# Forming the differences of a 16-bit split on TensorE instead of GpSimd, in the node stage ahead of attention

## The chip, the cores and the metric
One core of a Trainium2 chip runs the whole program in one launch. The metric is the device time of one execution in microseconds (us), where lower is better. A core has five engines with in-order instruction streams: TensorE (PE: matmuls and transposes, results go to PSUM), VectorE (DVE), ScalarE (ACT), GpSimd (POOL) and SyncE (SP, which issues DMAs). They are ordered only by semaphores that the kernel writes out by hand.

## The reference, cut to what matters
A network of two layers over 3125 nodes of 256 channels and 50000 edges. The change lies between the mixture of experts of layer 0 and the residual sum behind the attention of layer 1:

```python
# layer 0: y = x + (two chosen experts, weighted); then a layer norm with gamma and beta is added
x = x + (layernorm(y) * gamma + beta)
# layer 1, attention over edges, on the normalized nodes
h = (layernorm(x) @ W.T).reshape(n, 8, 32)
alpha = (h[src] * a_src).sum(-1) + (h[dst] * a_dst).sum(-1)
alpha = alpha + (relu(edge_attr @ edge_W.T + edge_b) * h[dst]).sum(-1)
...
x = x + segment_sum(h[src] * attn) + bias
x = x + ffn(layernorm(x))
```

## The kernel before
The nodes are padded to NT = 25 tiles of P = 128 rows, one row per partition, in TURNS = 5 turns of TB = 5 tiles. The program is a row of blocks with a barrier of all engines between two; inside a block every engine has its own function. `nodes1` (the stage in front of attention) is one such block, `attention` is the next, and `hidden1` (last node stage and first half of the feed-forward network) the one behind.

In `nodes1` the engines do this. SP issues the loads (three per turn: the results of the two experts and the normalized nodes, 640 KB each), between them three broadcasts of small vectors (`a_src`, `a_dst`, bias), and then the stores of 25 finished rows. DVE: the products that append the attention columns to the weights (L1484, L1485), then `combine(c)` of a turn (weighted sum of the loads, L1453 and L1454, and statistics), `update(c)` (L1464, L1465: the normalized sum is added to x, and statistics of x) and `offsets(c)` (L1472), in the order combine(0), combine(1), update(0), and then for each turn c: combine(c+2), offsets(c), update(c+1). ACT takes square roots (`root`, L906) for both norms, normalizes five tiles at once (`apply`, L1544) when offsets(c) is done, and then, tile by tile, copies the transposed tile out of PSUM (`copy_turned`, L1551), copies the product out (`take`, L1558) and makes three 16-bit parts of it. PE transposes each tile (`turn`, L1508) and multiplies it with the weights (`project`, L1517, 272 columns, f32).

The three parts are: part 0 is the row rounded to bf16 (L1560, from the copied row in SBUF, so it waits for that copy); the first difference, row minus part 0, is formed by GpSimd (`rests`, L1615) or, in the last turn, by DVE (`late_rests`, L1478); part 1 is that rounded (L1564); the second difference is formed by GpSimd (`lefts`, L1619); part 2 is that rounded (L1568, a whole turn later). The parts go to `hparts`, which attention reads; the row goes to a table in DRAM, from which attention gathers.

GpSimd also adds beta to all of x ahead of the turns (L1605, five instructions of 128x1280), adds the bias of attention's output to x after each turn's five tiles (`with_bias`, L1609, 128x1280) and clears the turn's part of `acc` (L1622), into which attention writes and which served as a load buffer until then. ACT issues `again.root(c + 1)` behind the five tiles of turn c, and offsets(c+1) on DVE waits for it: so a turn's tiles on ACT and PE lie in a ring with the next turn's offsets.

In `hidden1` (turns of CT = 4 tiles) DVE runs nodes(0), nodes(1), normalized(0), and then alternates. `nodes(c)` is per tile: attention's sums times the inverse denominator (L1771), added to x (L1773), statistics (L890). PE starts with the transposes of the first normalized tile (L1802), then the large products (L1811).

## Time and profile before
| | us |
|---|---|
| median of 3 runs | 2664.62 (2662.47 to 2669.9) |
| the profiled execution | 2668.54 |
| its span, first to last instruction | 2666.6 |
| of it `nodes1`, 1367 to 1520.4 | 153.4 |
| `attention`, 1520.4 to 2194.7 | 674.3 |
| `hidden1` up to 2345 | 150.3 |

All later times are microseconds from the start of the span. The median of the runs is 3.9 us below the profiled execution, 0.15% of it. Busy time of an engine counts the union of its instructions; "x4" is a count of instructions.
### The profile page before, as it was taken

The page shows a single profiled execution, that of the slowest core. Times are in us where ns is not written, and L with a number is a line of the kernel's source. Part 1 is how long each engine was busy: PE and PEld are TensorE (multiplying, and loading weights), DVE is VectorE, ACT ScalarE, POOL GpSimd, SP SyncE. Part 2 cuts the span into 40 slices and gives each one's busy share as a digit, 9 for nine tenths or more (in the row PEclk, how much of TensorE's full clock was granted, in tenths as well). Part 3 has the DMA queues.
Part 4 walks back from the last instruction along what each step waited for, and adds up shares of the span by engine and source line. Part 5 has one row for each costly group of instructions (what it writes and reads, how often), then busy time and mean ns, then how long its engine had stood idle before and what let it go on. Part 6 is the DMA issues. An engine that isn't in the chain of part 4 may idle for free. (4 is left out here: it accounts for less than half of the span.)

```text
span 2666.6 us, 41224 instructions
## 1 busy us (share of the span) xinstructions
PE 1931.2 (72%) x12513; PEld 1491.1 (56%) x12602; DVE 1654.7 (62%) x3320; ACT 918.3 (34%) x2309; POOL 1266.6 (47%) x1252
## 2 busy tenths in 40 slices
PE   3366666666269987499942578888888878969994
PEld 1245444444247765399931356666666652329994
DVE  8555555555257768655559589999999986031222
ACT  7333333323100002133313645555555543423331
POOL 0377777777710000155543577777777740002221
PEclk9678787777679998699976699999999998979997
DMA  2355554544478861522250255555555535000113
GB/s 78 104 183 188 193 175 167 179 162 164 146 270 284 293 223 50 177 70 72 70 183 21 87 153 160 163 158 162 161 164 162 162 91 174 18 8 31 38 38 112
DMA packets 192123, 366.13 MB, mean 137 GB/s; under 512 B 47573, under 2 KB 102632, under 8 KB 191525
## 3 DMA queue, kind: packets, MB, share of 16 engines
q1 hardware_dynamic: 135472, 207.05, 24.0%
q0 software_dynamic: 56160, 156.43, 18.6%
q8 instruction: 106, 1.74, 0.3%
q14 instruction: 111, 0.91, 0.1%
q10 hardware_dynamic: 274, 0.00, 0.0%
HBM read 232.23 MB, written 131.07 MB: 136 GB/s over the span
## 5 line engine op out<-in xcount | busy, mean ns | idle before, releaser
L1970 POOL DMA_INDIRECT att_rows<-hdram,top_ix x488 | 499.0, 1023 | 149.8 <-issue 147.7
L839 POOL DMA_INDIRECT mtab<-first_w,msgs_ix x308 | 308.2, 1001 | 93.9 <-issue 89.0
L708 PE MATMUL msgs_p_m<-nodes_n,msgs_hott 128*128 x976 | 316.3, 480 | 40.0 <-issue 31.0
L2040 PE MATMUL att_p_acc<-att_msg,att_hot 128*128 128x264 f32 x976 | 249.4, 400 | 77.2 <-ACT att_msg L2085 54.7
L708 PEld LDWEIGHTS msgs_p_m<-nodes_n,msgs_hott 128*128 128x128 f32 x976 | 221.3, 238 | 92.3 <-issue 56.2
L1141 POOL IOTA route_column<- 128x50 f32 (+1 forms) x2 | 0.3, 171 | 524.8 <-ACTq L1137 524.8
L2040 PEld LDWEIGHTS att_p_acc<-att_msg,att_hot 128*128 128x128 f32 x976 | 177.1, 191 | 119.7 <-DVE att_msg L2207 59.9
L1341 PE MATMUL exp_y<-exp_own,exp_ht 128*128 128x256 f32 x1032 | 239.0, 379 | 2.4 <-issue 2.4
L2070 ACT ACTIVATE att_enc<-att_p_z 128x1024 f32<-128x1024 f32 x122 | 124.8, 1023 | 298.3 <-PE att_p_z L1983 298.3
L839 POOL DMA_INDIRECT mtab<-msgs_rw,msgs_ix x180 | 181.6, 1009 | 72.7 <-issue 52.1
L1341 PEld LDWEIGHTS exp_y<-exp_own,exp_ht 128*128 128x128 f32 x1032 | 188.5, 190 | 24.7 <-issue 3.1
L607 DVE TENSOR_TENSOR first_w<-msgs_p_m,msgs_sorted 128x1024 f32<-128x1024 f32 x77 | 94.3, 1224 | 151.5 <-PE msgs_p_m L708 142.5
L1364 ACT COPY exp_xt<-exp_turned 128x256 f32<-128x256 f32 x97 | 36.1, 372 | 359.2 <-PE exp_turned L1320 359.2
L1285 DVE COPY exp_own<-ffn_w 128x2048 f32 x32 | 39.3, 1227 | 190.0 <-PE exp_y L1341 188.1
L2158 DVE TENSOR_TENSOR att_enc<-att_enc,att_p_h 128x1024 f32<-128x1024 f32 x122 | 148.7, 1218 | 12.8 <-PE att_p_h L1993 9.8
L2160 DVE TENSOR_REDUCE att_al<-att_enc 128x32 f32<-128x1024 f32 x122 | 148.8, 1220 | 4.2
L2207 DVE TENSOR_TENSOR att_msg<-att_rows,att_ex 128x1024 f32<-128x1024 f32 x122 | 148.8, 1219 | 1.1
L743 PE MATMUL msgs_p_m<-first_w,msgs_hott 128*128 128x256 f32 x616 | 143.2, 386 | 1.1 <-issue 0.3
L772 ACT CAST msgs_hott<-msgs_p_hot 128x512 f32<-128x512 bf16 x122 | 71.4, 585 | 179.3 <-PE msgs_p_hot L698 172.9
L1331 PEld LDWEIGHTS exp_hidden<-exp_xt,exp_own 128*128 128x128 f32 x1040 | 127.8, 194 | 4.5 <-issue 1.3
L1331 PE MATMUL exp_hidden<-exp_xt,exp_own 128*128 128x128 f32 x1040 | 128.3, 277 | 1.0 <-DVE exp_own L1277 1.0
L743 PEld LDWEIGHTS msgs_p_m<-first_w,msgs_hott 128*128 128x128 f32 x616 | 110.9, 189 | 32.2 <-issue 17.7
(390 smaller groups left out, 3966.3 us busy)
## 6 DMA issues: line engine op xcount, KB each, us to landing
first_w<-mtab SPq DMA_DIRECT2D x77, 520.0 KB, 4.6
etab<-msgs_et SPq DMA_DIRECT2D x122, 288.0 KB, 2.3
att_hz<-etab SPq DMA_DIRECT2D x122, 288.0 KB, 3.0
msgs_rw<-mtab SPq DMA_DIRECT2D x45, 520.0 KB, 4.7
first_w<-in_L_ffn_w SPq DMA_DIRECT2D x16, 512.0 KB, 4.6
ffn0x_w<-in_L_ffn_w SPq DMA_DIRECT2D x16, 512.0 KB
ffn_w<-in_L_ffn_Wd SPq DMA_DIRECT2D x8, 1024.0 KB, 12.1
att_rows<-hdram,top_ix POOLq DMA_INDIRECT x488, 3.2
```

Of the source, the lines that this page charges most:

```text
L607: V.tensor_tensor(rw[g % RS][:, :, 0:C], p_m[g % 2][:], bc(rows[:, g % SR, :, 6], 2, C), ALU.mult).then_inc(s_rw, 1)
L708: last = T.matmul(p_m[g % 2][:, q, :], hott[g % 2][:, q, :], node, start=True, stop=True)
L743: last = T.matmul(p_m[g % 2][:, 0, :], hott[g % 2][:, q, :], rw[g % RS][:, q, 0:C], start=(q == 0), stop=(q == G - 1))
L839: nc.gpsimd.indirect_dma_start(mtab, bass.IndirectOffsetOnAxis(ap=ix[:, g, q:q + 1], axis=0), rw[g % RS][:, q, :], None).then_inc(s_free[g ...
L1331: last = T.matmul(hidden[t % 2][:, f * P:(f + 1) * P], own1[:, k, f * P:(f + 1) * P], xt[t % 2][:, k * P:(k + 1) * P], start=(k == 0), sto ...
L1341: last = T.matmul(y[t % 2][:, 0:C], ht[t % 2][:, f, :], own2[:, f, :], start=(f == 0), stop=(f == FC - 1))
L1970: nc.gpsimd.indirect_dma_start(rows[:, g % RS, q, :], None, hdram, bass.IndirectOffsetOnAxis(ap=ix1[:, g, q:q + 1], axis=0)).then_inc(s_ro ...
L2040: last = T.matmul(p_acc[g % 2][:, 0:HW], hot[g % 2][:, q, :], msg[g % 2][:, q, :], start=(q == 0), stop=(q == G - 1))
L2070: S.activation(enc[g % 2][:], p_z[:], ACT.Relu).then_inc(s_enc, 1)
L2158: V.tensor_tensor(e[:], e[:], p_h[:], ALU.mult).then_inc(s_prod, 1)
L2160: V.tensor_reduce(al[t % 2][:, j * G:(j + 1) * G, :].rearrange("p q h -> p (q h)"), e[:].rearrange("p q (h d) -> p (q h) d", h=H), AX, ALU ...
L2207: V.tensor_tensor(msg[g % 2][:].rearrange("p q (h d) -> p q h d", d=D + 1)[:, :, :, 0:D], rows[:, g % RS, :, 0:C].rearrange("p q (h d) -> ...
```

## The change
The stage's split is reordered, and its pieces change engines:

- `rests`, `late_rests`, `lefts`, `with_bias` and `clear` leave GpSimd and DVE. GpSimd keeps only the five additions of beta.
- PE forms both differences in PSUM: `less_first(i)` is identity times row (f32) plus minus-identity times part 0 (bf16), `less_second(i)` is the same with parts 0 and 1 subtracted, in one bank (`p_left`), so it waits for the third part of the tile before. The bf16 matrix `minus` is made once by DVE.
- ACT reads the row's part 0 out of PSUM instead of out of the copied row, and the second and third part out of PSUM too; the third part follows three tiles behind, across turns, not a turn later. ACT also clears `acc`, one tile a time (`clear`, 128x264).
- PE's loop runs two tiles further and ACT's three, as a pipeline over all 25 tiles.
- On DVE combine(0) and combine(1) now come ahead of the products for the weights.
- The bias is loaded at the head of `hidden1` and added there by DVE, one more 128x256 addition per tile in `nodes`, which waits for that load once.

```diff
-            row_broadcast(sp, bi[:], A["L1_gnn_bias"], s_bi)
...
             V.memset(none[:], 0.0).then_inc(s_none, 1)
+            V.tensor_scalar(minus[:], cst["ident"][:], -1.0, None, ALU.mult).then_inc(s_minus, 1)
+            combine(0)
+            combine(1)
             dve.wait_ge(s_av, 32)
...
-            combine(0)
-            combine(1)
...
-            for i in range(LASTC, NT):
-                late_rests(i)
...
                 if i >= 2:
-                    pe.wait_ge(s_row, i - 1)
+                    pe.wait_ge(s_first, i - 1)
...
+            def less_first(i):
+                pe.wait_ge(s_first, i + 1)
+                if i >= 2:
+                    pe.wait_ge(s_second, i - 1)
+                T.matmul(p_less[i % 2][:, 0:HN], cst["ident"][:], row[i % 4][:, 0:HN], start=True, stop=False)
+                T.matmul(p_less[i % 2][:, 0:HN], minus[:], hparts[:, i, 0, :], start=False, stop=True).then_inc(s_less, 1)
+
+            def less_second(i):
+                pe.wait_ge(s_second, i + 1)
+                if i:
+                    pe.wait_ge(s_third, i)
+                T.matmul(p_left[0][:, 0:HN], cst["ident"][:], row[i % 4][:, 0:HN], start=True, stop=False)
+                T.matmul(p_left[0][:, 0:HN], minus[:], hparts[:, i, 0, :], start=False, stop=False)
+                T.matmul(p_left[0][:, 0:HN], minus[:], hparts[:, i, 1, :], start=False, stop=True).then_inc(s_left, 1)
...
-            for i in range(NT):
-                if i % TB < TB - 1:
+            for i in range(NT + 2):
+                if i % TB < TB - 1 and i + 1 < NT:
                     turn(i + 1)
-                project(i)
+                if i < NT:
+                    project(i)
+                if 0 <= i - 1 < NT:
+                    less_first(i - 1)
+                if 0 <= i - 2 < NT:
+                    less_second(i - 2)
...
                 S.copy(row[i % 4][:], p_o[i % 2][:, 0:HP]).then_inc(s_row, 1)
-                act.wait_ge(s_row, i + 1)
-                S.copy(hparts[:, i, 0, :], row[i % 4][:, 0:HN]).then_inc(s_first, 1)
+                S.copy(hparts[:, i, 0, :], p_o[i % 2][:, 0:HN]).then_inc(s_first, 1)
...
+            for i in range(NT + 3):
+                c, b = i // TB, i % TB
+                if b == 0 and i < NT:
+                    if c + 2 < TURNS:
+                        norm.root(act, S, c + 2)
+                    for k in range(TB):
+                        apply(c * TB + k)
+                if i < NT:
                     copy_turned(i)
+                if 0 <= i - 1 < NT:
+                    take(i - 1)
+                if 0 <= i - 2 < NT:
+                    second(i - 2)
+                if 0 <= i - 3 < NT:
+                    third(i - 3)
+                if b == TB - 1 and c + 1 < TURNS:
                     again.root(act, S, c + 1)
+                if i < NT:
+                    clear(i)
...
         @block.sync
         def _(sp):
+            row_broadcast(sp, bi[:], A["L1_gnn_bias"], s_bi)
             sp.dma_start(flat[:], A["L1_ffn_b1"].rearrange("(f p) -> f p", p=P)).then_inc(s_in, 16)
...
+                    link(V.tensor_tensor(to[:], to[:], bi[:], ALU.add))
                     link(V.tensor_tensor(x[:, i, :], x[:, i, :], to[:], ALU.add))
...
             link(V.reciprocal(den[:], den[:]))
+            dve.wait_ge(s_bi, 16)
             nodes(0)
```

## Rows read from the trace of the kernel before

**Rows 1.** Busy time by stage: stretch, length; busy us (x instructions) per engine; PEclk, DMA, GB/s.
```profile
1367.00:1520.40 153.40, 49.68 (x154) 33.71 (x154) 116.10 (x245) 58.43 (x162) 66.13 (x60) 0.61 0.27 90
1520.40:2194.70 674.30, 538.84 (x5097) 418.40 (x5186) 604.24 (x899) 350.41 (x704) 498.98 (x488) 0.98 0.54 156
```

**Rows 2.** Timeline, head of nodes1: start, duration, engine, line, operation, out<-in, [idle before].
```profile
1367.77 14.67 POOL L1605 TENSOR_TENSOR top_x<-top_x,wts_be 128x1280 f32<-128x1280 f32 x5 [4.79 <-POOLq L87]
1376.77 2.94 DVE L1484 TENSOR_TENSOR upd_tmp<-upd_w,upd_av 128x512 f32<-128x512 f32 x1 [8.63 <-DMA upd_av<-in_L_gnn_a_dst]
...
1383.87 0.48 DVE L1453 SCALAR_TENSOR_TENSOR sum_acc<-upd_got,wts_wt,sum_acc 128x256 f32<-128x256 f32 x1 [0.16 <-DVE upd_w L1485]
```

**Rows 3.** Timeline: update(0) begins on DVE; then apply(0) on ACT and update(1) on DVE.
```profile
1401.70 0.48 DVE L1464 SCALAR_TENSOR_TENSOR sum_acc<-sum_acc,upd_norm_mean,wts_ga 128x256 f32<-128x256 f32 x1
...
1419.72 2.57 ACT L1544 ACTIVATE upd_n<-top_x,upd_again_mean,upd_again_t 128x256 f32<-128x256 f32 x5
1419.82 0.49 DVE L1464 SCALAR_TENSOR_TENSOR sum_acc<-sum_acc,upd_norm_mean,wts_ga 128x256 f32<-128x256 f32 x1
```

**Rows 4.** Timeline, DVE and POOL behind the first turn's tiles.
```profile
1434.13 3.16 DVE L1453 SCALAR_TENSOR_TENSOR sum_acc<-upd_got,wts_wt,sum_acc 128x256 f32<-128x256 f32 x1
1434.13 2.88 POOL L1609 TENSOR_TENSOR top_x<-top_x,upd_bi 128x1280 f32<-128x1280 f32 x1
```

**Rows 5.** Timeline, from apply(3) to the last instruction of nodes1.
```profile
1484.12 2.08 ACT L1544 ACTIVATE upd_n<-top_x,upd_again_mean,upd_again_t 128x256 f32<-128x256 f32 x4 [2.98 <-DVE upd_again_mean L1472]
...
1498.17 0.20 ACT L906 ACTIVATE upd_again_t<-upd_again_var 128x5 f32<-128x5 f32 x1
...
1498.63 2.69 DVE L1472 SCALAR_TENSOR_TENSOR upd_again_mean<-upd_again_mean,upd_again_t 128x5 f32<-128x5 f32 x1
...
1501.36 2.56 ACT L1544 ACTIVATE upd_n<-top_x,upd_again_mean,upd_again_t 128x256 f32<-128x256 f32 x5 [2.98 <-DVE upd_again_mean L1472]
...
1504.23 2.18 PE L1517 MATMUL upd_p_o<-upd_w,upd_xt 128*128 128x272 f32 x4 [1.04 <-ACT upd_xt L1551]
...
1519.51 0.41 ACT L1568 CAST heads_parts<-upd_rest 128x264 bf16<-128x264 f32 x1 [0.23 <-POOL upd_rest L1619]
```

**Rows 6.** Timeline, costs of one piece: PE at full clock, and ACT back to back.
```profile
1428.41 0.38 PE L1508 MATMUL upd_p_t<-top_ident,upd_n 128*128 128x128 f32 x2
...
1428.63 1.08 PE L1517 MATMUL upd_p_o<-upd_w,upd_xt 128*128 128x272 f32 x4
...
1477.06 0.41 ACT L1564 CAST heads_parts<-upd_rest 128x264 bf16<-128x264 f32 x1
1477.37 0.36 ACT L1551 COPY upd_xt<-upd_p_t 128x256 f32<-128x256 f32 x1
...
1701.81 2.05 PE L2040 MATMUL att_p_acc<-att_msg,att_hot 128*128 128x264 f32 x8 [0.76 <-DVE att_msg L2207]
...
1704.43 1.47 PE L1993 MATMUL att_p_h<-wts_logits,att_hz 128*128 128x256 bf16 x12
```

**Rows 7.** Timeline of PE: the first matmul after an idle stretch in attention.
```profile
1543.38 0.33 PE L2009 MATMUL att_p_top<-top_ident,att_al 128*128 128x128 f32 x1 [3.58 <-DVE att_al L2173]
```

**Rows 8.** Busy time and granted clock right behind that idle stretch.
```profile
1544.00:1545.00 1.00, 1.00 (x4) 0.37 (x3) 0.96 (x2) 0.09 (x1) 0.70 (x2) 0.50 0.34 110
```

**Rows 9.** Timeline, hidden1: SP's first load, the first tile on DVE, PE's first transposes.
```profile
2194.73 0.35 SPq L1750 DMA_DIRECT2D hid_flat<-in_L_ffn_b  x1
...
2196.60 0.42 DVE L1771 TENSOR_TENSOR hid_part<-sum_acc,hid_den 128x256 f32<-128x256 f32 x1
...
2197.06 0.42 DVE L1773 TENSOR_TENSOR top_x<-top_x,hid_part 128x256 f32<-128x256 f32 x1
...
2210.87 2.33 PE L1802 MATMUL hid_p_t<-top_ident,nodes_n 128*128 128x128 f32 x8 [8.40 <-DVE nodes_n L914]
```

**Rows 10.** Busy time in hidden1 once PE runs.
```profile
2220.00:2345.00 125.00, 125.00 (x310) 39.49 (x309) 27.63 (x90) 49.48 (x81) 0.00 (x0) 1.00 0.14 48
```

**Rows 11.** The 25 stores of rows in nodes1 (132 KB each), from issue to landing.
```profile
DMA to landing us min/median/max: 1.7/1.7/3.7
```

More of the change, by code:

```diff
@@ L1396, in nodes1 @@
     n2 = [a.sb(f"n2{s}", [P, TB, C]) for s in two]
-    w, av, bi = a.sb("w", [P, KC, HP]), a.sb("av", [P, 2, C]), a.sb("bi", [P, C])
+    w, av, minus = a.sb("w", [P, KC, HP]), a.sb("av", [P, 2, C]), a.sb("minus", [P, P], BF16)
     tmp, none = a.sb("tmp", [P, KC, C]), a.sb("none", [P, HR])
@@ L1400, in nodes1 @@
     row = [a.sb(f"row{s}", [P, HP]) for s in range(4)]
-    rest = [a.sb(f"rest{s}", [P, HN]) for s in range(TB)]
     p_w = a.ps("p_w", [P, KC, C])
-    p_t, p_o = ([a.ps(f"{m}{s}", [P, 512]) for s in two] for m in ("p_t", "p_o"))
+    p_t, p_o, p_less, p_left = ([a.ps(f"{m}{s}", [P, 512]) for s in range(k)] for m, k in (
+        ("p_t", 2), ("p_o", 2), ("p_less", 2), ("p_left", 1)))
     norm, again = Norm(a, "norm"), Norm(a, "again")
-    (s_av, s_chain, s_none, s_pw, s_w, s_wa, s_shift, s_n, s_t, s_xt, s_o, s_row, s_first, s_rest, s_late, s_second, s_left,
-     s_third, s_zero, s_bi, s_sum, s_be, s_acc) = (a.sem(m) for m in (
-         "av", "chain", "none", "pw", "w", "wa", "shift", "n", "t", "xt", "o", "row", "first", "rest", "late", "second",
-         "left", "third", "zero", "bi", "sum", "be", "acc"))
+    (s_av, s_chain, s_none, s_pw, s_w, s_wa, s_shift, s_n, s_t, s_xt, s_o, s_row, s_first, s_less, s_second, s_left,
+     s_third, s_zero, s_be, s_clear, s_minus) = (a.sem(m) for m in (
+         "av", "chain", "none", "pw", "w", "wa", "shift", "n", "t", "xt", "o", "row", "first", "less", "second", "left",
+         "third", "zero", "be", "clear", "minus"))
     s_got, s_out = [a.sem(f"got{c}") for c in range(TURNS)], [a.sem(f"out{s}") for s in range(4)]
-    def rest_ready(eng, i):
-        if i < LASTC:
-            eng.wait_ge(s_rest, i + 1)
-        else:
-            eng.wait_ge(s_late, i - LASTC + 1)
     with nc.Block() as block:
@@ L1574, in _ @@
             again.root(act, S, 0)
-            for c in range(TURNS):
-                if c + 2 < TURNS:
-                    norm.root(act, S, c + 2)
-                for b in range(TB):
-                    apply(c * TB + b)
-                for b in range(TB):
-                    i = c * TB + b
-                    copy_turned(i)
-                    if b:
-                        take(i - 1)
-                    if c:
-                        third(i - TB)
-                    if b >= 2:
-                        second(i - 2)
-                take((c + 1) * TB - 1)
-                for b in range(TB - 2, TB):
-                    second(c * TB + b)
-                if c + 1 < TURNS:
+            act.wait_ge(s_none, 1)
@@ L1593, in _ @@
                     again.root(act, S, c + 1)
-            for i in range(LASTC, NT):
-                third(i)
+                if i < NT:
+                    clear(i)
+            act.wait_ge(s_clear, NT)
         @block.gpsimd
         def _(pool):
-            G_ = nc.gpsimd
-            def chunk(c):
-                return x[:, c * TB:(c + 1) * TB, :]
-            def first_offset(c):
-                G_.tensor_tensor(chunk(c), chunk(c), bc(wts["be"][:], 1, TB), ALU.add).then_inc(s_be, 1)
@@ L1621, in clear @@
-            def clear(c):
-                nc.gpsimd.memset(acc[:, c * TB:(c + 1) * TB, :], 0.0).then_inc(s_acc, 1)
-            for c in range(TURNS):
-                first_offset(c)
-            pool.wait_ge(s_bi, 16)
-            for i in range(NT):
-                if i < LASTC:
-                    rests(i)
-                if i >= 2:
-                    lefts(i - 2)
-                if i % TB == TB - 1:
-                    with_bias(i // TB)
-                    clear(i // TB)
-            for i in range(NT - 2, NT):
-                lefts(i)
@@ L1737, in hidden1 @@
         "chain", "in", "b1", "bt", "n", "t", "xt", "h", "ht", "g", "flip", "l"))
-    s_store = a.sem("store")
+    s_store, s_bi = a.sem("store"), a.sem("bi")
     def tiles(c):
```

33 lines of the change are left out of this document (10 added, 23 removed).

## The prediction
> **What bounds the kernel now.** I read the busy time by stage first [rows 1]. The change touches nodes1 (153.4 us) and hidden1; attention between them keeps its code. In nodes1 the reader is to see that no engine but DVE is near full: 116.1 of 153.4 us, against PE 49.7, ACT 58.4 and POOL 66.1, and that PE's mean clock is 0.61.
>
> The timeline of the stage tells why. Undisturbed, DVE needs 18.12 us from the start of update(0) to the start of update(1), which is one update, one combine and one offsets [rows 3]. From the first apply at 1419.72 to the last conversion, ended at 1519.92, there are 100.2 us [rows 3, 5]. Part of this is DVE being stretched: while POOL adds the bias to five tiles (2.88 us), DVE's addition of 256 columns, 0.48 us elsewhere, takes 3.16 and ends just behind POOL's [rows 2, 4]. The same happens to the last offsets, an instruction on 5 columns that takes 2.69 us, and ACT waits for it for 2.98 us [rows 5]. The last turn then runs from 1501.36 to 1519.92, 18.6 us, with GpSimd and DVE in its chain.
>
> So the stage is DVE with GpSimd's interference for the first three turns, and for the last two the ring of ACT, PE and GpSimd: the root at 1498.17 frees offsets(4), which frees the last turn.
>
> In hidden1, DVE works through eight tiles before PE's first transpose at 2210.87, and PE is then busy 125 of 125 us [rows 9, 10]. What is added on DVE ahead of 2210.87 moves the end; what is added behind is covered by PE.
>
> **The change part by part.** Call S(c) the moment at which apply(c) starts on ACT. Before, S(0) is 1419.7 and S(4) 1501.4 [rows 3, 5].
>
> *Start on DVE.* combine(0) need not wait for the broadcast of a_dst any more, only for the first three loads. They were issued ahead of it on the same queue, and the product waited until 1376.77 for the broadcast [rows 2]; I take 1376.8 for combine(0). But POOL's additions of beta run until 1382.44 (five, some 2.9 each), and rows 2 show what that does: the product issued at 1376.77 takes 2.94, one per addition of POOL. Two of the combine's additions get through by 1383.0, 1.0 us of work. Before, combine(0) started at 1383.87, so DVE is 0.9 + 1.0 = 1.9 ahead. The products and reductions for the weights now stand behind combine(1), undisturbed. A pair of them took 1.43 (from POOL's end at 1382.44 to 1383.87), so 2.8 for two, between combine(1) and update(0). S(0) comes 2.8 - 1.9 = 0.9 later, at 1420.6. The `minus` matrix falls into time in which DVE waits for loads. PE needs the weights only after S(0), so their later place costs nothing else.
>
> *DVE's turns.* With no bias, no difference and no clear on GpSimd, DVE runs at 18.1 per turn. S(1) = 1438.7, S(2) = 1456.8, if the ring of ACT and PE is not slower. The bounds are 18.1 and, with a root that comes late, the ring's time below. From S(2) to S(3) and from S(3) to S(4) DVE has only an update (about 9 us, half of 18.1) and waits for the root of the turn before: the ring decides.
>
> *TensorE's new work.* Per tile at full clock, from rows 6: two transposes 0.38; project 1.08; each f32 matmul of 264 columns is two of the instructions that took 2.05 for eight, 0.51; each bf16 one of 256 columns 1.47/12 = 0.12. less_first is 0.51 + 0.12 = 0.63, less_second 0.51 + 0.25 = 0.76. Sum 2.85. No row shows f32 and bf16 weights taking turns within one sum; the bounds are 0 (project and transposes follow each other in rows 6 with no gap, 0.22 between their starts) and 0.76, the idle that a wait for DVE's product cost in attention [rows 6]. I take 0.15, nearer to the closely packed rows: 3.0 per tile, where turn and project alone were 1.46.
>
> *ScalarE's.* Two instructions back to back start 0.31 apart [rows 6]. Per tile six of them (turned tile, row, three parts, clear), 1.9 us, and 0.51 of apply: 2.4 per tile, below PE's 3.0 and covered by it. In the pipeline each part waits for something that PE did an iteration earlier, and less_second's wait for the third part of the tile before finds it done while PE does the next transposes, product and first difference (2.1 us). Queued behind that wait on PE are the next tile's transposes; ACT's copy of them would be the first to feel it.
>
> *The ring.* From S(c) to the first project 2.87 (five applies and a copy) [rows 5]. Then 2.5 for that iteration without its transposes, three more tiles at 3.0, and 1.5 for the third part, root, reciprocal and offsets: T = 2.87 + 2.5 + 9.0 + 1.5 = 15.9. In S terms it is 4x + 3.9 with x the tile. Before, from apply(3) at 1484.12 to the root it took 14.1 us, and 3.2 more passed until apply(4), most of it behind GpSimd's addition [rows 5]: T replaces 17.3. S(3) = 1472.7, S(4) = 1488.6.
>
> *The tail.* 2.87 + 2.5 + 3 x 3.0 + 2.6 (the last tile has no transposes) = 17.0, then two more differences of the pipeline's end 1.4, a wait for the second part 0.2, the last difference 0.76 and the third part 0.6: 20.0. Stage end 1508.6 against 1519.92: **11.3 us less**.
>
> *The clock.* The first project of the last turn runs at half speed (2.18 against 1.08) [rows 5, 6], since PE had been idle long before it. An idle of 3.58 us in attention, and the clock was at 0.50 in the microseconds after it [rows 7, 8]; after an idle of 0.76 it was full [rows 6]. In the changed stage PE ends a turn's pieces 2.87 + 2.5 + 4 x 3.0 = 17.4 after S(c). While DVE sets the pace (18.1) it then idles 1.3 until the first apply is through (0.6), works 0.4 on the transposes and idles 1.8 until project; where the ring sets the pace (15.9) it still holds 1.5 us of the turn before and idles only 1.0. A start at the lower level lasted at most from 1422.6 (S(0) + 2.87) to the full-speed transposes at 1428.41 [rows 3, 6], 5.8 us of which half is lost; I take 2.5. I take the first start cold (hidden: its turn has fewer differences and DVE bounds it) and the last two warm.
>
> The Trainium skill (TensorE: Matmul & The Clock Gate, What's actually happening and HAM oscillation) says that the array falls back to 1.2 GHz when it goes idle, and that loops with a wait in each round can start every round cold. By it this change, which fills PE's gaps, would either cure that here or pay it with twice the work; that it pays is the second rival, priced from rows.
>
> *The bias in hidden1.* One more addition per tile at 0.46 start to start [rows 9]; eight tiles stand before PE's first transpose: 3.7. The other 17 fall into DVE's idle time beside a PE that is full [rows 10]. The load: DVE wants it at 2196.60; SP issues first at 2194.73 and a DMA of its size landed 1.7 to 3.7 after its issue [rows 9, 11], so the wait is 0 to 1.9; I take 0.7, near the median. Behind it on SP's queue the other loads slip by some 0.4, and PE had got them and sat idle for 8.40 before the first transposes [rows 9]. Together **4.4 us more**.
>
> *Sum.* -11.3 + 4.4 = -6.9. The profiled execution (2668.54; span 2666.6) would become 2661.6, and on the median scale, 3.9 lower, 2664.6 - 6.9 = **2657.7**.
>
> **The rivals.**
> 1. *TensorE's tile is cheaper and the stage gains more.* x = 2.85 makes T 15.3, so the end falls by 3 x 0.6, and the bias's wait may be 0: -6.9 - 1.8 - 0.7 = -9.4, 2655.2. If in addition GpSimd's additions did not hold combine(0), S(0) would be 5 earlier: 2650. The rows for the latter speak against it (2.94 us).
> 2. *The clock falls at every turn.* T becomes 18.4, the tail 22.5: S(2) 1457.1, S(4) 1493.9, end 1516.4; the stage gains 3.5, the bias takes 4.4: +0.9, 2665.5. For it: two idle stretches near each other at each head. Against it: neither is as long as the 3.58 of rows 7.
> 3. *TensorE becomes the bound, the slower end.* The end is S(1) + 3T + T + 4.1. It equals the old end less 4.4 when T is about 18.1; from there on the whole is slower than before, 0.4 us per 0.1. That takes a tile of 3.55 warm. At a tile of 3.55 and cold starts T = 20.6 and the end is 1438.7 + 82.4 + 4.1 = 1525.2: +5.3 + 4.4 = +9.7, 2674.3. It needs the switch between f32 and bf16 weights and the waits to cost over 0.6 a tile, and the clock as in 2.
> 4. *The change doesn't do what it says.* GpSimd's interference is not what stretches DVE. Then S(0) to S(3) stays at 64.4 us (1419.72 to 1484.12, 10.1 more than three undisturbed turns) [rows 3, 5], S(4) is 0.9 + 15.9 behind it at 1500.9, the stage ends at 1520.9, and the whole is 1.0 + 4.4 = 5.4 slower, 2670.0. Rows 4 speak against it, both instructions starting together and ending 0.3 us apart.
>
> **How the numbers follow.** The forecast, 2657.7 with its own range 2655 to 2662, has 0.47; rival 1 0.23, rival 2 0.19, rival 3 0.07, rival 4 0.04. A measurement of this kernel can tell about 0.3%, 8.0 us, from no change, so the lines are 2656.6 and 2672.6. Faster takes rival 1 and a quarter of the forecast's range: 0.36. Slower takes rival 3: 0.07. The rest, 0.57, is within 0.3%. The range for 8 in 10 goes from 2651 (most of rival 1) to 2668 (rival 2 with its spread).
>
> **What would show each step.** In the profile after: DVE's additions in nodes1 at 0.48 throughout and S(1) - S(0) near 18.1; GpSimd busy some 14.7 us in the stage; five PE groups per tile within 3.0 us at full clock, and the granted clock 1.00 at the first project of the last two turns; the stage ending near 1508.6; in hidden1 PE's first transpose 16.1 + 4.4 us behind the barrier's first instruction instead of 16.1. I am wrong if a tile takes over 3.5 on PE, if ACT waits in each iteration for PE and PE for ACT, or if attention, whose code is the same, changes its 674 us.

## The result, and the profile after

| | before | after |
|---|---|---|
| device us, median (lowest to highest) | 2667.13 (2662.47 to 2671.47) | 2658.29 (2653.45 to 2661.21) |
| runs, taken on one chip | 12 | 12 |
| profiled execution, us | 2668.54 | 2656.97 |
| its span, us; mean granted clock | 2666.6; 0.878 | 2655.2; 0.884 |

The ratio is 0.9964, with a 95% interval of 0.9956 to 0.9973: 9.6 us less, between 7.2 and 11.7 (the two medians differ by 8.8). The interval, 0.27% to 0.44%, lies across the 0.3% that a measurement was taken to tell. The forecast was 2657.7, and its range of 2651 to 2668 holds the time. That it came so near is in part luck: the gain of the sum, 6.9, was too small, and the kernel before, at 2664.6 by three runs, is at 2667.1 by twelve.

The busy time by stage of the kernel after answers to [rows 1]: stretch, length, busy us (x instructions) of PE, PEld, DVE, ACT and POOL, granted clock, DMA share, GB/s. The stretches are nodes1, attention, hidden1.

```profile
1369.50:1505.40 135.90, 70.39 (x329) 52.29 (x329) 93.64 (x242) 63.26 (x187) 14.60 (x5) 0.73 0.31 101
1505.40:2180.10 674.70, 539.44 (x5097) 418.25 (x5186) 605.46 (x899) 350.87 (x704) 501.25 (x488) 0.98 0.54 156
2180.10:2330.30 150.20, 128.78 (x315) 41.44 (x315) 61.48 (x183) 55.46 (x91) 0.00 (x0) 0.91 0.28 93
```

In nodes1 DVE is busy 22 us less for nearly the same instructions (242, before 245), GpSimd 14.6 us instead of 66.1, and PE 21 us more. Attention is as long as before.

For all that follows I cut every profile at the same places. S(c) is the moment at which apply(c) starts on ACT, as in the prediction. The tail runs from S(4) to the first instruction of the next stage. The head of hidden1 runs from DVE's first instruction to PE's first transposes, and "rest" from there to the end of the span.

| us | S(0) after the start | S(0) to S(4), turn by turn | tail | nodes1 | attention | head of hidden1 | rest |
|---|---|---|---|---|---|---|---|
| before | 51.8 | 23.3, 23.7, 17.4, 17.2 | 19.0 | 152.5 | 674.4 | 16.1 | 455.7 |
| after | 51.7 | 18.1, 18.1, 16.1, 13.4 | 18.2 | 135.7 | 674.8 | 21.0 | 454.0 |

The difference of the two spans, 11.4 us, is 16.8 less in nodes1, 4.9 more at the head of hidden1, and 0.5 of parts that the change doesn't touch (attention 0.4 more, the rest 1.7 less, and all that lies ahead of nodes1 1.8 more). This last part is scatter between two executions.

The applies are the rows to read first. Timeline of ACT after (start, duration, engine, line, operation, out<-in, idle before), the five applies and the last conversion of the stage:

```profile
1421.36 2.57 ACT L1551 ACTIVATE upd_n<-top_x,upd_again_mean,upd_again_t 128x256 f32<-128x256 f32 x5
...
1439.49 2.57 ACT L1551 ACTIVATE upd_n<-top_x,upd_again_mean,upd_again_t 128x256 f32<-128x256 f32 x5
...
1457.63 2.57 ACT L1551 ACTIVATE upd_n<-top_x,upd_again_mean,upd_again_t 128x256 f32<-128x256 f32 x5
...
1473.77 2.57 ACT L1551 ACTIVATE upd_n<-top_x,upd_again_mean,upd_again_t 128x256 f32<-128x256 f32 x5 [0.16 <-DVE upd_again_mean L1464]
...
1487.14 2.56 ACT L1551 ACTIVATE upd_n<-top_x,upd_again_mean,upd_again_t 128x256 f32<-128x256 f32 x5 [0.16 <-DVE upd_again_mean L1464]
...
1504.64 0.38 ACT L1574 CAST heads_parts<-upd_p_left 128x264 bf16<-128x264 f32 x1 [1.09 <-PE upd_p_left L1520]
```

The first three starts lie 18.13 and 18.14 apart, DVE's undisturbed turn. The last two lie 13.37 apart, and the wait ahead of them is 0.16 where it was 2.98 [rows 5]: the root, the reciprocal and the five-column offsets pass from DVE to ACT without being held. The last row's wait is for PE's last difference, where it was for GpSimd's.

PE's work on one tile, from the timeline of PE after:

```profile
1492.48 1.08 PE L1503 MATMUL upd_p_o<-upd_w,upd_xt 128*128 128x272 f32 x4
1493.40 0.61 PE L1511 MATMUL upd_p_less<-upd_row,top_ident 128*128 128x264 f32 x2
1493.84 0.28 PE L1512 MATMUL upd_p_less<-heads_parts,upd_minus 128*128 128x264 bf16 x1
1493.95 0.61 PE L1518 MATMUL upd_p_left<-upd_row,top_ident 128*128 128x264 f32 x2
1494.40 0.28 PE L1519 MATMUL upd_p_left<-heads_parts,upd_minus 128*128 128x264 bf16 x1
1494.51 0.28 PE L1520 MATMUL upd_p_left<-heads_parts,upd_minus 128*128 128x264 bf16 x1
1494.62 0.38 PE L1494 MATMUL upd_p_t<-top_ident,upd_n 128*128 128x128 f32 x2
1494.84 1.08 PE L1503 MATMUL upd_p_o<-upd_w,upd_xt 128*128 128x272 f32 x4
```

Read the starts, not the durations. From one project to the next is 2.36 us, though the durations of the seven groups add up to 3.52: each duration holds the end of a pipelined matmul, which the next one overlaps. Start to start, project costs 0.92, less_first 0.55, less_second 0.67, the transposes 0.22. There is no gap where f32 and bf16 take turns.

### The profile page after: what moved, and what is told of

Read it like the earlier page. It is cut to its first block and busy times, and to the rows that moved or that the text cites. A ratio compares the mean times of both kernels' runs of the same rounds, so it can differ in the third digit from the quotient of the medians.

```text
span 2655.2 us, 41592 instructions
## 1 busy us (share of the span) xinstructions
PE 1953.0 (74%) x12688; PEld 1510.7 (57%) x12777; DVE 1642.4 (62%) x3341; ACT 924.5 (35%) x2334; POOL 1220.2 (46%) x1197
## 5 line engine op out<-in xcount | busy, mean ns | idle before, releaser
L1945 POOL DMA_INDIRECT att_rows<-hdram,top_ix x488 | 501.2, 1027 | 270.2 <-issue 147.5
L1364 ACT COPY exp_xt<-exp_turned 128x256 f32<-128x256 f32 x97 | 36.2, 373 | 358.5 <-PE exp_turned L1320 358.5
L743 PEld LDWEIGHTS msgs_p_m<-first_w,msgs_hott 128*128 128x128 f32 x616 | 111.0, 189 | 32.2 <-issue 17.7
```

The costliest lines, as they stand in the source:

```text
L743: last = T.matmul(p_m[g % 2][:, 0, :], hott[g % 2][:, q, :], rw[g % RS][:, q, 0:C], start=(q == 0), stop=(q == G - 1))
L1945: nc.gpsimd.indirect_dma_start(rows[:, g % RS, q, :], None, hdram, bass.IndirectOffsetOnAxis(ap=ix1[:, g, q:q + 1], axis=0)).then_inc(s_ro ...
```

## The experiments

All of these ran on other chips than the comparison above. The kernel before needs 3009 to 3012 us there. Cutting the profiles shows that nodes1 and the head of hidden1 agree to 0.5 us between chips, and that the difference is in attention (the last section). So each experiment is read by its cut against these two, and its time against runs of the kernel before on its own chip. In the expectations, theory A is the account of the prediction with the sizes that the profile after had shown; "Theory B" or "rival" is another account that the same text describes. Of the 95% intervals for times, none is narrower than 9 us on these chips, so single terms are decided by the cuts.

| | S(0) | S(0) to S(4) | tail | nodes1 | head of hidden1 |
|---|---|---|---|---|---|
| before_again | 51.9 | 23.2, 23.7, 17.1, 17.1 | 19.0 | 152.0 | 16.0 |
| after_again | 51.7 | 18.1, 18.1, 16.1, 13.4 | 18.2 | 135.7 | 21.1 |
| b_bias_late | 51.9 | 21.0, 21.4, 13.8, 14.9 | 16.0 | 139.1 | 21.2 |
| a_bias_pool | 51.7 | 20.4, 20.8, 17.7, 16.9 | 18.2 | 145.7 | 16.1 |
| a_no_bias | 51.7 | 18.1, 18.1, 16.0, 13.4 | 18.2 | 135.5 | 16.1 |
| a_bias_tail | 51.7 | 18.1, 18.1, 16.3, 13.4 | 18.2 | 135.8 | 16.0 |
| a_beta_late | 49.6 | 18.1, 18.1, 13.4, 13.4 | 18.2 | 130.9 | 16.1 |
| a_fill | 51.7 | 18.1, 18.1, 13.4, 13.4 | 18.2 | 132.9 | 21.2 |
| a_pe_extra | 51.7 | 18.1, 18.1, 15.1, 15.1 | 20.7 | 138.9 | 22.0 |
| a_weights_first | 51.9 | 18.1, 18.1, 16.2, 13.4 | 18.2 | 136.0 | 20.8 |
| beta_late_fill | 49.7 | 18.1, 18.1, 13.4, 13.4 | 18.2 | 130.9 | 16.1 |

### The two kernels again

before_again and after_again are the two kernels unchanged.

> The kernel before itself, for its profile on the same chip. Theory A: the stages that the change touches do not depend on the chip, only on engines: nodes1 152.5 us from its first DVE instruction to attention's, apply to apply 23.3, 23.7, 17.4 and 17.2, hidden1's first transpose 16.1 behind its first DVE instruction; attention 880 to 890 instead of 674. Rival: these stages are longer too, and the differences read between profiles of two chips are not to be trusted.

> The changed kernel itself, timed on the same chip as the two runs beside it. The chip of the experiments took some 3010 us for the kernel before where the first took 2667, most of it in attention. The change moves nodes1 and hidden1 by -16.8 and +4.9 in the profiles, 11.9 together. Theory A (the rest is untouched): ratio 0.9955 if one execution takes 2667, 0.9960 if it takes 3010. Rival (attention, started earlier or from other rows' timing, gives part of it back): ratio nearer 1 by more than 0.001.

after_again took 2998.53 us against 3008.84, ratio 0.9967 (0.9952 to 0.9982): the same gain on another chip, 9.9 us where it was 9.6. The expectation's 0.9960 lies inside that interval. Of before_again there is a single execution (3018.24 us); only its cut is used.

### Which part of GpSimd's work mattered

The kernel before, with the bias added in hidden1 and the differences left on GpSimd:

```diff
             row_broadcast(sp, av[:, 1, :], A["L1_gnn_a_dst"].rearrange("h d -> (h d)"), s_av)
-            row_broadcast(sp, bi[:], A["L1_gnn_bias"], s_bi)
...
                 if i % TB == TB - 1:
-                    with_bias(i // TB)
+                    pool.wait_ge(s_n, (i // TB + 1) * TB)
                     clear(i // TB)
...
+                    link(V.tensor_tensor(to[:], to[:], bi[:], ALU.add))
                     link(V.tensor_tensor(x[:, i, :], x[:, i, :], to[:], ALU.add))
```

> The kernel before with one part of the change alone: GpSimd no longer adds the bias in nodes1; it is loaded and added in hidden1 as in the changed kernel. The differences stay on GpSimd. Theory A (GpSimd's bias instruction stops DVE once per turn): four stalls of some 2.7 us between S(0) and S(4) and 2.9 in the tail go, 13.5 us off nodes1, and 4.9 come back before PE's first transpose in hidden1 (the changed kernel's trace has 21.0 us there against 16.1): 8.6 us faster than before, ratio 0.9968, nearly the whole of the change. Theory B (the gain comes from the differences on PE and the short pipeline): at most 3 us off nodes1 and 4.9 back, ratio 1.000 to 1.001.

It took 3001.66 us against 3009.42, ratio 0.9980 (0.9964 to 0.9996). Nodes1 went from 152.5 to 139.1: 13.4 less for the five instructions of bias alone, as A said (13.5). The cuts are not even, though: 2.3, 2.3, 3.5, 2.3 and 3.0 us from S(0) on, and PE's clock, which came back to 1.00 at other moments than in the kernel before, is in them too. What is left of the stretching shows in the first two turns, 21.0 and 21.4 instead of 18.1. The timeline of this kernel, DVE and POOL in the first turn:

```profile
1554.14 0.43 DVE L890 BATCH_NORM_STATS2 upd_again_st<-top_x 128x6 f32<-128x256 f32 x1
1554.49 0.68 POOL L1614 TENSOR_TENSOR upd_rest<-upd_row,heads_parts 128x264 f32<-128x264 f32 x1 [43.30 <-ACT heads_parts L1559]
1554.60 0.85 DVE L1463 SCALAR_TENSOR_TENSOR sum_acc<-sum_acc,upd_norm_mean,wts_ga 128x256 f32<-128x256 f32 x1
1555.49 0.48 DVE L1464 SCALAR_TENSOR_TENSOR top_x<-sum_acc,upd_norm_t,top_x 128x256 f32<-128x256 f32 x1
```

The addition that starts inside GpSimd's difference takes 0.85 instead of 0.48; the next one is free again. Added up over DVE's instructions, its busy time is 2.8 us more in the first turn and 3.3 more in the second than in those turns of after, which is what they are longer by.

The counterpart is the kernel after with the bias back on GpSimd, and not in hidden1:

```diff
             pool.wait_ge(s_be, TURNS)
+            pool.wait_ge(s_bi, 16)
+            for c in range(TURNS):
+                pool.wait_ge(s_n, (c + 1) * TB)
+                pool.wait_ge(s_second, c * TB + 3)
+                to = x[:, c * TB:(c + 1) * TB, :]
+                nc.gpsimd.tensor_tensor(to, to, bc(bi[:], 1, TB), ALU.add).then_inc(s_sum, 1)
+            pool.wait_ge(s_sum, TURNS)
```

> The changed kernel with the bias back on GpSimd, one instruction of 128x1280 behind each turn's tiles, and out of hidden1; the differences stay on PE. Theory A: GpSimd's instruction stops DVE again, 2.7 us each in turns 0 to 3 (twice an addition on the path, twice the small offsets instruction), so nodes1 takes 135.5 + 10.8 = 146.3, hidden1 gets 4.9 back: 5.9 slower than the changed kernel, ratio to before 0.9987. Theory B (the differences on GpSimd were what stretched DVE): no stall that matters, 4.9 faster than the changed kernel, ratio 0.9945.

It took 3002.71 us against 3009.42, ratio 0.9981 (0.9965 to 0.9997); nodes1 is 10.0 longer than after (A: 10.8), and the head of hidden1 4.9 shorter. Turn by turn it is 2.3, 2.7, 1.6 and 3.5 longer, where A had 2.7 for each: in the last of them the clock fell as well, which it doesn't do there in after (shown below). How such an instruction reaches ACT is in its timeline around S(3):

```profile
1602.43 2.90 POOL L1620 TENSOR_TENSOR top_x<-top_x,upd_bi 128x1280 f32<-128x1280 f32 x1 [17.75 <-ACT heads_parts L1573]
...
1603.31 2.04 DVE L1467 SCALAR_TENSOR_TENSOR upd_again_mean<-upd_again_mean,upd_again_t 128x5 f32<-128x5 f32 x1
...
1605.39 1.09 ACT L1554 ACTIVATE upd_n<-top_x,upd_again_mean,upd_again_t 128x256 f32<-128x256 f32 x2 [2.03 <-DVE upd_again_mean L1467]
```

GpSimd's addition ends at 1605.33. The offsets, five columns, are held to 1605.35, and the apply starts behind them at 1605.39. The Trainium skill (SBUF — State Buffer, "Who interferes with whom") says that a VectorE instruction with two inputs in SBUF contends with a GpSimd instruction that reads SBUF, for a port pair that one of them locks. These rows agree, and add that an instruction of five columns is held just as one of 256 is [rows 4].

Both runs price the parts, and the price depends on the order. From before, the bias instruction on GpSimd is worth 13.4 of the 16.8; the rest of the change, made on top of that, brings only 139.1 - 135.7 = 3.4, since it frees DVE of some 6 us in the first two turns but loads PE. In b_bias_late the turn between S(2) and S(3) took 13.8 and the tail 16.0; after, 16.1 and 18.2. In the other order, with the bias left on GpSimd, the rest is worth 152.5 - 145.7 = 6.8 (a_bias_pool against before), and taking the bias off then brings the 10.0. In both orders the bias is the greater part.

### The bias in hidden1

The kernel after without the bias: its load, its wait and its 25 additions are left out, so that the bias is missing from what this kernel computes.

```diff
-            row_broadcast(sp, bi[:], A["L1_gnn_bias"], s_bi)
...
-                    link(V.tensor_tensor(to[:], to[:], bi[:], ALU.add))
...
-            dve.wait_ge(s_bi, 16)
```

> The changed kernel with the bias left out of the computation everywhere, its load and its 25 additions. What the bias costs in hidden1 is then measured by itself. Theory A (eight additions and the wait for the load stand before PE's first transpose, the other 17 are hidden): hidden1's first transpose 16.1 us behind the stage's first DVE instruction, nodes1 unchanged at 135.5, 4.9 us faster than the changed kernel, ratio to before 0.9945. Rival (later turns of hidden1 are delayed too, since the square root of a turn waits on DVE): over 7 us faster.

It took 2991.27 us, ratio 0.9941 (0.9919 to 0.9964). The head of hidden1 is 16.1 again, 4.9 to 5.0 less, and nothing else moved. The timeline of the kernel after shows the two terms:

```profile
2180.12 0.33 SPq L857 DMA_DIRECT2D hid_bi<-in_L_gnn_bias  x1
...
2180.55 1.40 DVE L1757 RECIPROCAL hid_den<-hid_den 128x200 f32<-128x200 f32 x1
...
2183.24 0.43 DVE L1744 TENSOR_TENSOR hid_part<-sum_acc,hid_den 128x256 f32<-128x256 f32 x1 [1.29 <-DMA hid_bi<-in_L_gnn_bias]
2183.71 0.42 DVE L1746 TENSOR_TENSOR hid_part<-hid_part,hid_bi 128x256 f32<-128x256 f32 x1
...
2201.20 2.33 PE L1777 MATMUL hid_p_t<-top_ident,nodes_n 128*128 128x128 f32 x8 [11.82 <-DVE nodes_n L914]
```

DVE idles 1.29 for the load, which landed 3.0 us after its issue, and pays eight additions at 0.46. PE's idle before the transposes grew from 8.40 [rows 9] to 11.82.

Then the same work elsewhere: the bias added by DVE in nodes1, behind its last offsets, in five instructions of 1280 columns, and not in hidden1.

```diff
                 if c + 1 < TURNS:
                     update(c + 1)
+            dve.wait_ge(s_bi, 16)
+            for c in range(TURNS):
+                dve.wait_ge(s_n, (c + 1) * TB)
+                to = x[:, c * TB:(c + 1) * TB, :]
+                V.tensor_tensor(to, to, bc(bi[:], 1, TB), ALU.add).then_inc(s_sum, 1)
+            dve.wait_ge(s_sum, TURNS)
```

> The changed kernel with the bias added by DVE in nodes1, in five instructions of 128x1280 behind offsets(4), and out of hidden1. DVE was idle for the last 18.3 us of nodes1 in the changed kernel's trace; the additions are 5 of some 1.35 us, 6.8 us. With GpSimd idle nothing stops them. Theory A: nodes1 stays at 135.5, hidden1 gets its 4.9 back, ratio to before 0.9945, faster than both kernels. Rival (the long DVE instructions hold up the last turn, because ACT or PE read x or SBUF beside them): the tail from S(4) grows over its 17.9 us and part of the 4.9 is lost.

It took 2996.18 us, ratio 0.9945 (0.9926 to 0.9964). The five additions are there (1.49 us each) and lie in the tail, where DVE has nothing left to do: nodes1 135.8, head of hidden1 16.0. The bias is free there.

### The clock, and PE's load

After S(2) the ring took 16.1 where it took 13.4 after S(3). The timeline of PE after, at the head of turn 2 and at that of turn 4:

```profile
1458.29 0.93 PE L1494 MATMUL upd_p_t<-top_ident,upd_n 128*128 128x128 f32 x4 [2.64 <-ACT upd_n L1551]
1460.51 2.18 PE L1503 MATMUL upd_p_o<-upd_w,upd_xt 128*128 128x272 f32 x4 [1.29 <-ACT upd_xt L1558]
...
1490.01 1.19 PE L1503 MATMUL upd_p_o<-upd_w,upd_xt 128*128 128x272 f32 x4 [1.28 <-ACT upd_xt L1558]
```

and the granted clock in the same places (the third number from the end of each line; columns as in the busy time by stage):

```profile
1457.00:1459.00 2.00, 0.66 (x4) 0.41 (x4) 1.83 (x8) 1.58 (x4) 0.00 (x0) 1.00 0.00 0
1459.00:1461.00 2.00, 0.71 (x3) 0.49 (x2) 1.86 (x5) 2.00 (x7) 0.00 (x0) 0.59 0.00 0
1461.00:1463.00 2.00, 2.00 (x6) 1.43 (x6) 1.86 (x5) 1.43 (x6) 0.00 (x0) 0.50 0.24 76
1489.00:1491.00 2.00, 0.99 (x4) 0.87 (x5) 0.00 (x0) 2.00 (x8) 0.00 (x0) 1.00 0.00 0
```

At turn 2 PE idled 2.64 us, worked 0.93 on the transposes, idled 1.29, and the clock stood at 0.50 (1.2 GHz) for the first project (2.18). At turn 4 it idled only the 1.28, and the clock stayed at 1.00 (2.4 GHz). The other four profiles whose work up to there is the same in this respect (after_again, a_no_bias, a_bias_tail and a_weights_first) have the fall at turn 2 as well, behind idles of 2.45 to 2.76 and 1.29 us, and turns of 16.0 to 16.3. Was the fall what made turn 2 long, or had PE too much to do? a_fill puts matmuls of no use into the two idle stretches:

```diff
+            def fill(n):
+                for _ in range(n):
+                    T.matmul(p_w[:].rearrange("p k c -> p (k c)")[:, 0:HN], minus[:], hparts[:, 0, 0, :], start=True, stop=True)
...
+                    if i + 1 == 2 * TB:
+                        fill(12)
                     turn(i + 1)
+                    if i + 1 == 2 * TB:
+                        fill(14)
```

> The changed kernel with 26 bf16 matmuls of 264 columns on PE into a free PSUM bank, 12 ahead of the transposes that open turn 2 and 14 behind them. They compute nothing that is used; they fill the idle stretch in which the granted clock fell to 0.50 in the changed kernel. Theory A (that fall is what makes turn 2 longer than turn 3, 16.1 against 13.4 us from apply to apply): the clock stays at 1.00, S(2) to S(3) becomes 13.4, nodes1 2.7 us shorter, 132.8 against 135.5. Rival (turn 2 is longer because DVE is busy with update(3) beside it): the clock stays up and the 16.1 remain.

S(2) to S(3) fell from 16.1 to 13.4, and nodes1 to 132.9 (A: 132.8). In the timeline of PE of this kernel the project that had taken 2.18 takes 1.18:

```profile
1583.67 1.51 PE L1524 MATMUL upd_p_w<-heads_parts,upd_minus 128*128 128x264 bf16 x12
1586.31 0.44 PE L1494 MATMUL upd_p_t<-top_ident,upd_n 128*128 128x128 f32 x2 [1.12 <-ACT upd_n L1559]
1586.58 1.74 PE L1524 MATMUL upd_p_w<-heads_parts,upd_minus 128*128 128x264 bf16 x14
1588.16 0.38 PE L1494 MATMUL upd_p_t<-top_ident,upd_n 128*128 128x128 f32 x2
1588.54 1.18 PE L1503 MATMUL upd_p_o<-upd_w,upd_xt 128*128 128x272 f32 x4
```

So the fall of the clock at turn 2 costs 2.8 us (16.13 to 13.37). There is a single execution of it (2996.39 us), as of a_pe_extra (3002.83) and a_weights_first (2994.14), so these three are read by their cuts alone.

The other question was whether T = 4x + 3.9 holds, with x PE's time for a tile. a_pe_extra does the first f32 product of less_first twice:

```diff
+                T.matmul(p_less[i % 2][:, 0:HN], cst["ident"][:], row[i % 4][:, 0:HN], start=True, stop=True)
                 T.matmul(p_less[i % 2][:, 0:HN], cst["ident"][:], row[i % 4][:, 0:HN], start=True, stop=False)
```

> The changed kernel with the first f32 product of every first difference done twice, 0.46 us more on PE per tile at full clock; the result is the same. Theory A (DVE sets the pace up to S(2), PE from there on): S(0) to S(1) and S(1) to S(2) stay at 18.1, S(3) to S(4) grows by 4 x 0.46 = 1.8 to 15.2, the tail by 6 x 0.46 = 2.8 to 20.7, S(2) to S(3) by 1.8 to 2.3: nodes1 6.4 to 6.9 us longer. Rival (the waits between ACT and PE set the pace, not PE's work): under 2 us longer. Second rival (PE sets the pace everywhere): 25 x 0.46 = 11.5 longer.

S(3) to S(4) grew from 13.4 to 15.1, 1.8 us: four times the 0.44 of one more product. The tail grew by 2.4 (A: 2.8). But S(2) to S(3), where A had expected it to grow too, became 15.1, a whole microsecond less than after. The timeline of PE says why:

```profile
1592.86 0.93 PE L1494 MATMUL upd_p_t<-top_ident,upd_n 128*128 128x128 f32 x4 [0.42 <-ACT upd_n L1552]
1595.08 1.18 PE L1503 MATMUL upd_p_o<-upd_w,upd_xt 128*128 128x272 f32 x4 [1.29 <-ACT upd_xt L1559]
```

PE came so late out of turn 1 that it idled only 0.42 before the transposes, and the clock stayed up. That miss of A supports the account of the clock: more work, less time, and the 15.1 are the 13.4 of a warm turn and the same four products as in the next. PE's load is thus on the path from S(2) on, at four tiles per turn.

The idle stretches do not say by themselves when the clock falls. a_bias_pool has the same ones at the heads of turns 3 and 4:

```profile
1606.04 0.93 PE L1497 MATMUL upd_p_t<-top_ident,upd_n 128*128 128x128 f32 x4 [1.36 <-ACT upd_n L1554]
1608.26 1.27 PE L1506 MATMUL upd_p_o<-upd_w,upd_xt 128*128 128x272 f32 x4 [1.29 <-ACT upd_xt L1561]
1609.32 1.09 PE L1514 MATMUL upd_p_less<-upd_row,top_ident 128*128 128x264 f32 x2
...
1622.95 0.93 PE L1497 MATMUL upd_p_t<-top_ident,upd_n 128*128 128x128 f32 x4 [1.36 <-ACT upd_n L1554]
1625.18 1.18 PE L1506 MATMUL upd_p_o<-upd_w,upd_xt 128*128 128x272 f32 x4 [1.29 <-ACT upd_xt L1561]
1626.20 0.61 PE L1514 MATMUL upd_p_less<-upd_row,top_ident 128*128 128x264 f32 x2
```

At turn 3 the granted clock fell to 0.50 while PE was at work, 3.9 us behind S(3), and stayed there for 3.4 us (the first difference took 1.09 instead of 0.61); at turn 4 it stayed at 1.00. In a_pe_extra it fell at turn 1 behind 2.23 and 1.29. What decides between such cases, these runs don't show.

### Order, and GpSimd's additions of beta

a_weights_first puts the products for the weights ahead of combine(0) again:

```diff
-            combine(0)
-            combine(1)
             dve.wait_ge(s_av, 32)
...
             dve.sem_inc(s_wa, 1)
+            combine(0)
+            combine(1)
             update(0)
```

> The changed kernel with the products for the weights ahead of combine(0) and combine(1), as before the change. The prediction held that the new order puts S(0) 0.9 us later; the changed kernel has it 51.8 us behind the stage's start against 52.0 before. Theory A (both orders lose one gap to each of GpSimd's additions and differ only in how much of DVE's own work fits beside them): S(0) at 51.9 to 52.2, nodes1 0.1 to 0.4 us longer. Rival (the new order is worth what combine(0) did ahead of time, two additions and more): S(0) over 1 us later.

S(0) is 0.2 later, nodes1 136.0 against 135.7, as A said: the order is worth 0.3 us at most, in one profile.

The last known interference is that of GpSimd's five additions of beta at the start. a_beta_late is a_bias_tail, with the last of them kept back until the statistics of turn 3 are done:

```diff
             for c in range(TURNS):
+                if c == TURNS - 1:
+                    pool.wait_ge(again.s_var, c)
                 to = x[:, c * TB:(c + 1) * TB, :]
```

> The kernel with the bias added by DVE behind offsets(4), and in addition GpSimd adds beta to the last turn's rows only after the statistics of turn 3, when DVE waits for ACT's root, not at the head of the stage. Theory A: GpSimd's fifth instruction at the head held one of combine(0)'s additions for some 2.1 us; S(0) comes 2.1 to 2.5 earlier than 51.8 us behind the stage's start, the later addition (2.9 us) lies in DVE's wait of some 4 to 6 us and holds nothing, nodes1 takes 133.4, ratio to before 0.993. Rival: the instruction at its new place holds the small offsets instruction, as the bias did before: S(4) comes up to 2.7 later and nothing is won.

It took 2994.06 us against 3011.86, ratio 0.9941 (0.9921 to 0.9961; the cuts give 0.9928). S(0) came 2.1 earlier, and nodes1 is 130.9, where A said 133.4. The further 2.5 are turn 2, which began at full clock here: turn 1's start was at half clock for longer (its second project took 1.59 where it took 1.08 after), PE came later out of it, and idled 1.42 and 1.29 us at the head of turn 2 instead of 2.64 and 1.29. That this was enough to keep the clock up is not shown: behind 1.36 and 1.29 it did both in a_bias_pool. The addition itself starts where DVE has no update left (timeline of POOL):

```profile
1588.98 2.90 POOL L1621 TENSOR_TENSOR top_x<-top_x,wts_be 128x1280 f32<-128x1280 f32 x1 [83.52 <-DVE upd_again_var L901]
```

beta_late_fill is this kernel with the fill of a_fill:

> The kernel with the bias behind offsets(4) and the last turn's beta late, and in addition the 26 idle matmuls that hold PE's clock at the head of turn 2. Without them this kernel's profile had the clock up at turn 2 by itself (13.4), where others had 16.0 to 16.3. Theory A: nodes1 130.9 again, with the clock at 1.00 from turn 1's end on, hidden1's first transpose at 16.1, ratio to before 0.993 at 3010 us (21.6 of stage time), 0.992 at 2667. Rival (the fill delays the first product of turn 2): S(2) to S(3) over 14.

It took 2989.13 us against 3008.84, ratio 0.9927 (0.9901 to 0.9953), and 9.4 less than after_again on the same chip, where the cuts give 4.8 in nodes1 and 5.0 in hidden1. It beats the kernel before clearly; against after the six runs say it less firmly (the two intervals of the ratio just touch), and the cuts, 9.8 us, bear it out. The fill added nothing here, since turn 2 was at full clock without it in a_beta_late; as code it is the safer of the two, since without it the clock at turn 2 may go either way.

## Why the prediction was right, and which terms were off

The direction, the stages and the mechanism were as forecast: DVE free of GpSimd at 18.1 per turn, the ring behind it for the last two turns, and the bias on the path in hidden1. Each term, in the order of the prediction:

| term | forecast | measured | |
|---|---|---|---|
| S(0) | +0.9 | -0.2 | 1.1 too late |
| S(0) to S(2) | 36.2 | 36.3 | right |
| S(2) to S(3) | 15.9, warm | 16.1, cold | two misses that cancel |
| S(3) to S(4) | 15.9 | 13.4 | 2.5 too long |
| S(4) to the last conversion's end | 20.0 | 17.9 | 2.1 too long |
| nodes1 | -11.3 | -16.8 | |
| hidden1: eight additions | 3.7 | 3.7 | right |
| hidden1: wait for the load | 0.7 | 1.3 | 0.6 too short |
| sum | -6.9 | -11.9 | |

The sum of the measured terms, 11.9, is 0.2 beyond the interval of the first comparison (7.2 to 11.7) and inside that of after_again (5.4 to 14.4). What of it doesn't reach the 9.6, 2.3 us, stays open: parts that nobody changed differ by up to 1.8 us between the two profiles of the first chip, and attention by 11 between those of before_again and after_again (890.9 and 879.6).

*The mis-sized term is PE's tile.* I took 3.0 us. Measured are 2.36: the transposes 0.22 and project 0.92 start to start, the differences 0.55 and 0.67, the switch 0. My 0.38 and 1.08 were durations of [rows 6], with the drain that the next matmul overlaps. The same rows gave the starts (1428.41 and 1428.63, 0.22 apart), and I read them so for the gap but not for the cost. Of the 0.64, the transposes and project have 0.16 each, the two differences 0.17 together and the switch 0.15. With x = 2.36 the prediction's own T = 4x + 3.9 gives 13.3, and 13.37 was measured; a_pe_extra then confirmed the factor 4. Cut into the prediction's parts, that turn is 2.88, 2.25, 7.09 and 1.15 us, where it had 2.87, 2.5, 9.0 and 1.5: so 2.15 of the 2.5 are PE's, and 0.35 are the way from PE's last difference over root and offsets to the next apply. This is rival 1 in its mechanism, and further than it went (x = 2.85).

*The clock.* I took the last two turns warm and they were, and the first start cold. The ring of turn 2 I also priced as warm, and it was cold; that its 15.9 met the measured 16.1 is luck, a tile too dear and a clock too fast. Turn 1 began at half clock too (idles of 4.00 and 1.04 us, then 0.50 up to 6.2 us behind S(1)), which DVE's 18.1 us hide. Its head had been described (an idle stretch, the transposes, an idle of 1.8), with the first idle at 1.3 on the strength of the 3.0 us tile. With 2.36 per tile PE was done earlier and idled 2.64. So the cheaper tile gave back 2.8 us there, by a_fill; rival 2, a fall at every turn, was right for turns 0 to 2 and wrong for 3 and 4, which the ring paces and which have only one idle of 1.28 us. The question of the prediction, whether filling PE's gaps cures the cold starts or pays for them, has both answers: before, the clock stood at 0.50 for the first 8 to 9 us of every turn, and after it does so at the heads of turns 0 to 2, up to 7.3, 6.2 and 8.6 us behind S(c), and not in the last two. What that is worth within the 16.8 us no run separates. The Trainium skill (TensorE: Matmul & The Clock Gate, "What's actually happening") says that an array that goes idle is gated back to 1.2 GHz. The rows at turn 2 agree. They add that the clock fell there behind two stretches, neither as long as the 3.58 of [rows 7], with 0.93 us of transposes between them; behind 1.42 and 1.29 it stayed up, and behind 1.36 and 1.29 it did once the one and once the other.

*S(0).* combine(0) began 8.1 us behind the stage's first instruction on DVE, where I had put it at 8.9, and got three additions and a statistics instruction through GpSimd's five instead of two additions. Timeline of the kernel after:

```profile
1377.76 0.64 DVE L1445 SCALAR_TENSOR_TENSOR sum_acc<-upd_got,wts_wt,sum_acc 128x256 f32<-128x256 f32 x1 [5.23 <-DMA sum_acc<-ntab]
1378.44 2.99 DVE L1446 SCALAR_TENSOR_TENSOR sum_acc<-upd_got,wts_wt,sum_acc 128x256 f32<-128x256 f32 x1
1381.46 0.43 DVE L890 BATCH_NORM_STATS2 upd_norm_st<-sum_acc 128x6 f32<-128x256 f32 x1
1381.92 2.53 DVE L1445 SCALAR_TENSOR_TENSOR sum_acc<-upd_got,wts_wt,sum_acc 128x256 f32<-128x256 f32 x1
1384.48 0.48 DVE L1446 SCALAR_TENSOR_TENSOR sum_acc<-upd_got,wts_wt,sum_acc 128x256 f32<-128x256 f32 x1
```

The pace, one held addition per addition of GpSimd's, was as taken from [rows 2]; the first one here, 0.64, was hardly held. From 1384.48 on every addition of 256 columns takes 0.47 to 0.49, as was asked of this profile.

*The wait for the load.* Bounds of 0 to 1.9 were given and 1.29 measured; I had gone near the median of 1.7 us of stores in the middle of a stage [rows 11], and this load, the first of its block, took 3.0. In a_pe_extra it took 4.0 and the wait was 2.24, in a_weights_first 2.8 and 1.11, so the upper bound of 1.9 was too low as well.

*Rivals 3 and 4.* For PE to make the whole slower took a tile of 3.55: it costs 2.36. That GpSimd doesn't stretch DVE fell by S(0) to S(2), and b_bias_late and a_bias_pool show it both ways.

Two small slips of its arithmetic change nothing here: rival 1 and a quarter of the forecast's range are 0.35 and not 0.36, and 64.4 us are 10.0 more than three undisturbed turns and not 10.1.

## What to carry to other kernels

Price work on TensorE by the distance between starts of groups that follow each other, not by their durations; with four groups a tile the difference was a fifth of the tile. When an engine is relieved, ask separately for each part of what it did: here five long instructions of bias were worth 13.4 us and everything else that moved 3.4 on top of it (10.0 and 6.8 in the other order), since the differences' new place was on a path too. And an addition that has to be made somewhere belongs where its engine has run out of work (DVE behind its last offsets), which made 4.9 us of cost into nothing.

## What was not expected of the hardware

- PE's granted clock fell after idle stretches of 2.64 and 1.29 us with 0.93 us of transposes between them, and not after 1.42 and 1.29, 0.42 and 1.29, or 1.28 alone. After 1.36 and 1.29 it fell at one turn of a_bias_pool and not at the next, so these lengths alone don't decide. A fall cost 2.8 us in this ring. More work on PE (a_pe_extra) made that turn faster by 1.0.
- f32 and bf16 weights take turns within one accumulation without a gap: two f32 instructions of 264 columns 0.44 to 0.45, a bf16 one 0.11, start to start.
- An instruction of DVE on five columns, 0.17 us when free (a_beta_late), took 2.04 us, to the end of GpSimd's addition (a_bias_pool).
- The same kernel needs 3009 us on these other chips where the first had 2667. Nodes1 is equal to 0.5 us, attention takes 880 to 891 instead of 674. The costliest group of the page (busy us, mean ns | idle us before them) is the gathers by GpSimd. On the page of after, on the first chip:

```profile
L1945 POOL DMA_INDIRECT att_rows<-hdram,top_ix x488 | 501.2, 1027 | 270.2 <-issue 147.5
```

and on that of after_again:

```profile
L1945 POOL DMA_INDIRECT att_rows<-hdram,top_ix x488 | 510.9, 1047 | 452.9 <-issue 315.3
```

The instructions are as long (1027 and 1047 ns), but GpSimd stands idle 183 us more ahead of them, 168 of it (315.3 - 147.5) without a releaser in the profile. What holds it was not tried; the comparison of the two kernels comes out the same on either chip.
